# Two weight chunks stored ahead of the late weights, and the weights of the second attention prepared in the order keys, queries, values, outputs

## What is computed

```python
x = L0_attn_x                                  # (8, 256, 256)
xn = _layernorm(x, axis=-1)
x = x + _L0_attn_ref(xn, ...) + _L0_ffn_ref(xn, ...)
xn = _layernorm(x, axis=-1)
x = x + _L1_attn_ref(xn, ...) + _L1_ffn_ref(xn, ...)
return x
```

```python
def _mxfp4_matmul(x, codes, scales, block_size=BLOCK):
    w = codes * jnp.repeat(scales, block_size, axis=0)
    return x @ w
...
scores = jnp.einsum('bqhd,bkhd->bhqk', q, k) / jnp.sqrt(jnp.float32(HEAD_DIM))
```

## Time and profile before

| | us |
|---|---|
| median of 3 runs | 1114.13 |
| lowest and highest run | 1113.35 to 1114.25 |
| the profiled execution, whole | 1113.54 |
| its span in the trace | 1111.8 |
| PE busy in the span | 1046.6 (94%) |
| DVE busy | 840.2 (76%) |
| ACT busy | 687.6 (62%) |
| POOL busy | 519.5 (47%) |

### The profile page before, as it was taken

How to read it: one execution, slowest core, us unless ns; L and a number is a source line. 1 busy time by engine, 2 the same in 40 slices (tenths; PEclk the granted TensorE clock), 3 DMA queues, 4 the chain that set the end, 5 groups by cost and what they waited for, 6 DMA issues and landing times.

```text
span 1111.8 us, 21342 instructions
## 1 busy us (share of the span) xinstructions
PE 1046.6 (94%) x7339; PEld 956.7 (86%) x7339; DVE 840.2 (76%) x1696; ACT 687.6 (62%) x1922; POOL 519.5 (47%) x626
## 2 busy tenths in 40 slices
PE   8768899899899799999999999999999999999997
PEld 6657779779778688888899999999999999899997
DVE  6676787887867667887777777778777777777776
ACT  3856676766665435555666666766666665555554
POOL 5586665664675000007844454444453443588200
PEclk9999999999999999999999999999999999999999
DMA  7746746746664296624544554445445453333130
GB/s 219 230 129 193 215 142 204 202 153 190 176 211 138 91 261 175 220 87 157 173 139 139 150 203 148 149 134 158 161 140 177 147 163 99 106 100 97 65 114 19
DMA packets 140490, 171.71 MB, mean 154 GB/s; under 512 B 11232, under 2 KB 103520, under 8 KB 139488
## 3 DMA queue, kind: packets, MB, share of 16 engines
q1 hardware_dynamic: 137312, 161.96, 47.7%
q0 software_dynamic: 3072, 8.39, 2.3%
HBM read 121.95 MB, written 48.37 MB: 153 GB/s over the span
## 4 chain that ended last, share of the span: by engine, by line
PE 64%; DVE 13%; POOL 8%; ACT 6%; DMA 4%; issue 3%; SPq 2%; DVEq 0%; POOLq 0%; ACTq 0%
PE ps_m L1703 25%; PE ps_s L1703 9%; PE ps_t L1703 7%; PE ps_b L1703 4%; PE ps_b L849 3%; POOL d_xs L1332 3%; ACT probs L502 2%; PE ps_t L1858 2%; PE ps_c L1858 2%; PE ps_c L1703 2%; DMA d_w_head<-parts 2%; DVE neg_max L791 2%; PE ps_t L916 1%; PE ps_m L849 1%; DMA d_q_scr<-sT 1%
## 5 line engine op out<-in xcount | busy, mean ns | idle before, releaser
L1450 ACT ACTIVATE probs_a<-ps_s,neg_max_a 128x256 f32<-128x256 f32 x256 | 118.0, 473 | 139.6 <-DVE neg_max_a L1667 139.6
L1703 PE MATMUL ps_m<-xTa,w_qk 128*128 128x512 f32 x768 | 199.0, 398 | 4.2 <-DVE v L1519 1.6
L1703 PEld LDWEIGHTS ps_m<-xTa,w_qk 128*128 128x128 f32 x768 | 136.8, 188 | 34.7 <-issue 5.4
L502 ACT ACTIVATE probs<-ps_s,neg_max 128x128 f32<-128x128 f32 (+1 forms) x256 | 104.9, 422 | 55.4 <-DVE neg_max L791 54.2
L1667 DVE TENSOR_REDUCE neg_max_a<-ps_s 128x2 f32<-128x512 f32 x128 | 87.9, 690 | 43.3 <-PE ps_s L1703 41.7
L1349 POOL CAST we_down<-raw_down_e 128x256 fp32r<-128x256 f32 x47 | 18.7, 398 | 208.5 <-DMA raw_down_e<-in_we_down 208.5
L1703 PE MATMUL ps_m<-w_v,xTa 128*128 128x256 f32 x768 | 106.1, 288 | 0.0
L1703 PE MATMUL ps_s<-kTa,qTa 128*128 128x256 f32 x768 | 102.9, 283 | 0.3 <-DVE kTa L1489 0.2
L1703 PE MATMUL ps_t<-pTa,v 128*128 128x256 f32 x762 | 102.8, 284 | 0.0
L1703 PEld LDWEIGHTS ps_s<-kTa,qTa 128*128 128x128 f32 x768 | 96.7, 192 | 1.0 <-DVE kTa L1489 0.7
L1703 PEld LDWEIGHTS ps_t<-pTa,v 128*128 128x128 f32 x762 | 96.2, 191 | 0.1
(11 more groups left out here) (261 smaller groups left out, 2827.9 us busy)
## 6 DMA issues: line engine op xcount, KB each, us to landing
w_qk<-d_w_head SPq DMA_DIRECT2D x64, 512.0 KB, 3.9
raw_up<-in_we_up SPq DMA_DIRECT2D x47, 352.0 KB, 3.6
d_w_head<-parts SPq DMA_DIRECT2D x128, 128.0 KB, 2.6
raw_down_e<-in_we_down SPq DMA_DIRECT2D x47, 256.0 KB, 2.9
codes<-in_w_codes SPq DMA_DIRECT2D x64, 128.0 KB
scales<-in_w_scales SPq DMA_DIRECT2D x64, 128.0 KB
q<-d_q_scr SPq DMA_DIRECT2D x28, 256.0 KB, 5.3
d_xs<-zeros SPq DMA_DIRECT2D x16, 384.0 KB, 5.6
```

The lines of the kernel that those rows point to most:

```text
L502: last = act.activation(probs[:, g % 3, a * w:(a + 1) * w], ps_s[g % 2][:, a * w:(a + 1) * w], ACT.Exp, bias=neg_max[:, g % 2, a:a + 1], s ...
L1450: last = act.activation(probs[:, s, t, :], ps_s[s][:, t * SEQ:(t + 1) * SEQ], ACT.Exp, bias=neg_max[:, s, t:t + 1], scale=1.0, accum_out=s ...
L1703: last = pe.matmul(out, lhs[i], rhs[j], start=start and n == 0, stop=stop and n == 2, skip_group_check=True)
```

## The change

Two edits. The weights are prepared in the order of `ORDER = (1, 0, 2, 3)`: keys in turn 0, queries in turn 1, values and outputs in turns 2 and 3 as before. The multiplication of the scales, which only queries have, goes from the 16 splits of turn 0 to those of turn 1. And SP issues the chunks 0 and 1 (two waits, four stores, four loads) ahead of the late weights instead of in steps 0 and 1; the transfer of zeros that belonged to chunk 0 gets a function of its own and stays where it was.

```diff
+    ORDER = (1, 0, 2, 3)
...
-            m, half, at = n // CHUNKS, n % CHUNKS // (CHUNKS // 2), n % (CHUNKS // 2) * PC
+            m, half, at = ORDER[n // CHUNKS], n % CHUNKS // (CHUNKS // 2), n % (CHUNKS // 2) * PC
...
+        def clear(i):
+            sp.dma_start(dram["xs"].rearrange("(u t p) n -> u p t n", u=4 * TURNS, p=P)[i],
+                         zeros[:].unsqueeze(1).to_broadcast([P, CLEARED, D])).then_inc(cleared, 16)
+
         def chunk(n):
 
-            m, half, h = n // CHUNKS, n % CHUNKS // (CHUNKS // 2), n % (CHUNKS // 2) * (PC // HD1)
-            if n % 4 == 0:
-                sp.dma_start(dram["xs"].rearrange("(u t p) n -> u p t n", u=4 * TURNS, p=P)[n // 4],
-                             zeros[:].unsqueeze(1).to_broadcast([P, CLEARED, D])).then_inc(cleared, 16)
+            m, half, h = ORDER[n // CHUNKS], n % CHUNKS // (CHUNKS // 2), n % (CHUNKS // 2) * (PC // HD1)
+            if n % 4 == 0 and n:
+                clear(n // 4)
...
         load_q(0, 1)
+        for n in range(2):
+            chunk(n)
         late_loads = [(raw_down, "w_down"), (raw_o, "w_o"), (raw_s2, "w_s2"), (raw_gw, "w_gw"), (raw_s13, "w_s13")]
...
         sp.wait_ge(zero_ok, 1)
+        clear(0)
         for g in range(ALL):
...
-            if chunk_of(p, n) is not None:
+            if chunk_of(p, n) is not None and (p or chunk_of(p, n) >= 2):
...
-            if n < CHUNKS:
+            if ORDER[n // CHUNKS] == 0:
                 pool.tensor_scalar(scales[:, a, :], scales[:, a, :], HD1 ** -0.5, None, ALU.mult).then_inc(scaled, 1)
-                pool.wait_ge(scaled, n + 1)
+                pool.wait_ge(scaled, n % CHUNKS + 1)
```

## The result

The changed kernel takes 1116.8 us (median of 6 runs, 1115.92 to 1117.88) where the kernel before takes 1113.29 (median of 6 runs): the ratio is 1.0035, with a 95% interval of 1.0024 to 1.0045. It is slower by 3.5 us by the medians and 3.9 by the ratio; forecast was a gain of 1.7. The profiled execution took 1115.92 us, with a span of 1114.2.

A forecast was written before the change was run, and what follows sets the result against it. It took POOL's wait for chunk 0's store, delaying turn 0's last hidden tile and PE, as the bound to remove. Terms -1.8 - 1.4 + 0 + 1.5 + 0 = -1.7 us gave 1112.4 us, range 1110.3 to 1114.9.

The forecast's parts named there:

- What bounds the kernel, turn 0: POOL's 8.81 us pause for chunk 0's store delays the last hidden tile; PE waits 1.78 us before the first out.
- Turn 0, -1.8 - 1.4: At the first out item PE gains 1.8 us of waiting, and 1.4 us by running it at full clock.
- The clock term: First out item of turn 0 takes 2.15 us instead of 3.56: 1.4 us gained, bounds 0 and 1.4.
- Late weights, 0: Late weights, queued behind chunks 0 and 1, land near 39.7 us, before ACT needs them at 42.12: cost 0.
- The rival: Late weights land at 44.9 us, ACT stops 2.8 us, PE's clock falls for 1.4 more: 1116.6 us, chance 0.09.
- Turn 1, +1.5 with bounds 0.9 and 2.85: Longer splits in turn 1 cost 1.5 us: 1.1 through the late inverse root, 0.4 through SP's query stores.
- most of this falls into pauses of POOL: Turn 1's 16 splits get 1.05 us longer each, 16.8 us in all, mostly absorbed while POOL waits.
- the forecast's 2.1 us: Splits of chunks 30 and 31 in turn 1, 1.05 us longer each, make the following rstd 2.1 us later.
- Slack from turn 2: End of turn 1: as turn 2's 1.86 us more wait cost 0.87, the 2.1 us delay costs 1.1.
- The term for the ports: DVE slowed beside POOL: 16.8 us less POOL work in turn 0, 16.8 more in turn 1; 0, with 0.5 either way.
- The sum: Whole kernel: -1.8 - 1.4 + 0 + 1.5 + 0 = -1.7 us, giving 1112.4 us.
- What would show it: Trace signs: turn 1 span about 89.4 us; wrong if ACT waits at 42 us, clock falls elsewhere, span stays 88.

The follow-up runs named there:

- changed, store first: Changed kernel with SP issuing, in turn 1, the store of chunk 28 ahead of the load of turn 2's queries: 1148.52 against 1143.80 us, ratio 1.0037.
- changed, bias later: Changed kernel with POOL adding turn 1's output bias in step 14 instead of 11: 1116.35 us against 1112.76 for the kernel before, ratio 1.0035.
- Two multiplications alone: Kernel before with multiplications by 1.0 added in the splits of chunks 30 and 31 of turn 1: 1145.72 against 1144.32 us, ratio 1.0009.

## Why the prediction was wrong, step by step

**What bounds the kernel, turn 0: right.** POOL's pause of 8.81 us is gone (0.80 is left), the last hidden tile ends at 67.7 and not near 66 as forecast, and PE does not wait for it.

**Turn 0, -1.8 - 1.4: right in the trace, partly by chance.** From 66 to 74 us PE gained 3.5 us on the first trace. That the lead at 131 us is 3.19, nearly the forecast's 3.2, is luck: PE was 1.1 us behind at 66 and gained another 0.8 from 74 to 131, and the forecast had neither. And the long pause with the half clock behind it is in two of the five traces with this turn 0: against the second trace of the kernel before the changed kernel is 2.9 and 2.2 us ahead at the first shared tile. The clock term was read from one execution and is worth 0.3 to 1.4 us. The Trainium skill, page "TensorE: Matmul & The Clock Gate", section "What's actually happening", ties the gate to how busy PE has been recently, and says that runs of one kernel differ in how long its start is at half clock. The traces agree with the first where the clock falls behind pauses (2.20 us at 197 us here), and show the second further on in the kernel as well: the same program had its second stretch at half clock from 71 or from 78 us.

**Late weights, 0: wrong, small.** The step that failed here is "the total work is the same, and behind the late weights now stand only the input of turn 1 and the zeros: they land near 39.7". They were issued 6.85 us later and landed 6.6 later (44.5), 8.8 us from issue, 9.0 before: for this last transfer, on which all wait, the time from issue to landing hardly shrank (for the other five it did, by 0.2 to 2.0 us). DMA moved some 2.1 MB from 30 to 38 us, 2.8 in the kernel before; why is open. The rival put them at 44.9. Its price of 2.8 + 1.4 did not come up in the changed kernel, where PE was late at 37 us, ACT waited 0.52 us and DVE came to them at 44.5; it came up in part in the two kernels where PE's clock had not yet fallen (changed, store first, and changed, bias later: 2.21 and 1.30 us of DVE's wait, and PE at half clock from 46 us on). With the stores behind the late weights instead (old order, 130.07 against 130.99) turn 0 ends 0.9 us earlier, in one trace of each.

**Turn 1, +1.5 with bounds 0.9 and 2.85: wrong, 5.5 to 6.7.** This is the step that turned the sign. What failed is "most of this falls into pauses of POOL", with what was worked out from it: chunk 27 ready "about 1.9 us later", the second query store "0 to 0.75 us" later, of which 0.4 were taken. In its place the runs showed:

- *The chain into the root.* Counted from the start of the turn, the store of chunk 27 is issued 3.2 us later, the second query store 2.2, and the query loads, which wait for its landing, 3.2 (it takes 1.0 us longer); split 30 starts 3.7 us later. The term for all this was 0.4. The two splits of the forecast's 2.1 us take 1.8 (0.9 us each more, where 1.05 was taken). So the root comes 5.5 us later, and DVE, itself 1.3 us later at this place, waits 0.26 + 5.5 - 1.3 = 4.5 us; forecast were 2.1 to 2.9 with 1.0 us of slack. PE loses 4.4 us from 191 to 220 us, part of it at half clock (198 to 205 us). With the root ahead of the two splits 4.3 us of the turn are gone, since the root then waits neither for this chain nor for them.
- *Slack from turn 2.* "Of my 2.1 us the first 1.86 cost 0.87" compared the lengths of two turns that differ in more than this wait. Two multiplications alone cost 1.6 us of 1.8. In turn 2 the wait was worth 1.8 us until `cT`, which is late next there. Against the chain this is the smaller error, 0.5 us.
- *The rest of the turn*, which had no term: 1.8 us from 147 to 178. Half of it is `var_eps` behind the bias (the 0.6 us it took in the kernel before was the same collision, shorter), the other half lies in POOL's full stretch from 151 to 174, where the kernel before still had pauses of 1.7 and 4.8 us. That POOL's stretch is the cause of this half is argued from the rows and was not tested by a run. The term for the ports, 0 with 0.5 either way, was a sum over both turns and missed that one alignment can cost 0.9, or 2.4 where PE's clock falls behind it.

**The sum.** Put right: turn 0 -3.2, turn 1 +6.1, second layer -0.5: +2.4, which is the difference of the two spans. The forecast had -3.2, +1.5 and 0. The -0.5 is about what two traces of the kernel before differ by in the second layer (0.4). The medians differ by 3.5, as the profiled execution of the changed kernel lies 0.9 under its median.

**The rival on the slower side** had the late weights as its mechanism. The real one, the longer splits of turn 1 with the inverse root behind them, was in the text as a term of the sum and was never priced as a rival.

**What would show it.** The forecast named the span from the first shared tile of turn 1 to that of turn 2, "about 89.4", and being wrong "if the clock falls elsewhere". Both signs came up: 94.07, and the clock at 31 to 37 and at 198 us. The third, a wait of ACT for the late weights, came up with 0.52 us.

## What to carry to other kernels

Work moved from one turn to the next must be placed in the list of the engine that gets it, with its pauses counted stretch by stretch, and every transfer that is issued behind its results must be followed to the engine that waits for it: here POOL is busy for less than half of the time, and yet 0.9 us more in each split brought the last inverse root of the turn 5.5 us later, through two stores that follow each other and the two splits behind them. Short work put ahead of something small that another engine waits for costs nearly its full length, and a wait of another turn is a poor measure for it if something else is late there. Count such positions from the start of the turn in both kernels: in absolute time a lead and a delay can cancel, and the same time then looks like a fixed one. Here the cheapest edit was to leave the order alone and to store the chunks behind what is more urgent, 1.9 us; putting the small root ahead of two large splits may add to it in a turn where nothing else is late.

## What the runs showed of the hardware

- A DVE instruction on 128x2 numbers, 0.17 us long, took 1.50 us and ended at 144.87, when POOL's addition of 128x1024 (142.46 to 144.84) ended. In all seven traces with all 16 multiplications in turn 1 and the addition in step 11 it was 1.50 to 1.52; in the kernel before, where it came later beside the addition, 0.59; with the addition moved to step 14 it was 0.17, and with it in step 8, 0.54. (With step 8 POOL's addition is long over, at 135.6, and a short split instruction ends beside `var_eps`, at 144.18 against 144.22.) The Trainium skill, page "SBUF — State Buffer", section "Who interferes with whom", states that DVE and GpSimd share a port pair and that in DVE's two-port modes the later of the two is blocked until the other's instruction is over. The times agree with that; no run shows in which mode `var_eps` was.
- Early in the first layer PE's clock was at 1.2 GHz for 3 to 10 us in every trace, within 29 to 34, 29 to 41 or 46 to 54 us; the kernel before had the first in one trace and the second in another. At 29 to 34 us it costs next to nothing (the two traces without a fall before 46 us are no earlier at 37 us), at the second place 1.3 to 2.6 us, and the delay is partly cover for a later wait.
- The last of the six late weights took 9.0 us from issue to landing, and 8.8 when it was issued 6.85 us later, behind 1 MB more; the other five took 7.5 to 9.1 us, and then 6.1 to 7.3. What that time consists of stays open.
- In two of the four groups of runs the second layer took 30 us more, in all kernels, with PE's clock at 0.50 for 31 to 38 us from about 520 us on. One of these groups carries the same chip number as a group without it, so it is not a matter of the chip alone. Its cause was not looked for.
